# Weight parts in the weight's own column order, every fourth column as TensorE's stationary operand

## The reference, cut to what matters

```python
x = x + modulated(x, cond, w0)        # ((x * ys) @ w0) * d
x = x + rnn(x, h0=cond, Wx, Wh, b)    # h = tanh(h @ Wh + x @ Wx + b)
x = x + adapted(x, cond, base, ...)   # x @ (base + A_b B_b^T), A_b and B_b of rank 8, from cond
x = x + lstm(x, h0=cond, Wx, Wh, b)   # i, f, o, g of (x @ Wx + h @ Wh + b), 128 steps
```

## Time and profile before

| | |
|---|---|
| time, median of 3 runs | 1249.93 us (1248.52 to 1251.83) |
| the profiled execution | 1248.96 us, of which the span from the first to the last instruction is 1247.2 us |
| TensorE, matmuls | 1155.6 us busy, 93% of the span, 22740 matmuls and as many weight loads |
| VectorE | 877.9 us, 70% |
| ScalarE | 478.1 us, 38% |
| granted TensorE clock | 0.976 of full speed over the span |
| TensorE from 181 to 1140 us | 951.05 us busy of 959.00 |

### The profile page before, as it was taken

How to read it: one execution, slowest core, us unless ns; L and a number is a source line. 1 busy time by engine, 2 the same in 40 slices (tenths; PEclk the granted TensorE clock), 3 DMA queues, 4 the chain that set the end, 5 groups by cost and what they waited for, 6 DMA issues and landing times.

```text
span 1247.2 us, 50735 instructions
## 1 busy us (share of the span) xinstructions
PE 1155.6 (93%) x22740; PEld 755.4 (61%) x22740; DVE 877.9 (70%) x2483; ACT 478.1 (38%) x1148; POOL 55.4 (4%) x89
## 2 busy tenths in 40 slices
PE   4565699999999999999999999999999999999985
PEld 2452366666666666666666666666666666666642
DVE  6667577777777777777777777777777777776653
ACT  4366333334333333333433333333433333334332
POOL 1000000000000000000000000000000000000000
PEclk9787699999999999999999999999999999999999
DMA  8955000000000000000000000000000000000000
GB/s 301 369 217 161 1 16 9 17 19 20 20 19 20 19 20 9 13 20 20 20 20 19 20 20 12 12 18 20 20 19 20 19 20 19 10 4 11 11 11 18
DMA packets 49065, 51.00 MB, mean 41 GB/s; under 512 B 5984, under 2 KB 38752, under 8 KB 47184
## 3 DMA queue, kind: packets, MB, share of 16 engines
q1 hardware_dynamic: 48848, 47.77, 12.2%
HBM read 39.36 MB, written 8.39 MB: 38 GB/s over the span
## 4 chain that ended last, share of the span: by engine, by line
PE 46%; DVE 29%; ACT 14%; issue 9%; SPq 0%; DVEq 0%; ACTq 0%; DMA 0%; POOL 0%; POOLq 0%
PE ps_gates L1254 15%; PE ps_gates L1246 14%; PE ps_x L1186 7%; ACT rows L479 4%; PE ps_rnn L1270 3%; DVE gates_ring L935 3%; ACT gates_ring L581 2%; DVE lstm_hT L946 2%; PE ps_lr L1186 2%; DVE late L924 2%; PE ps_rnn L1273 2%; ACT x L479 2%; DVE x_ring L787 2%; PE ps_z L1186 2%; DVE x1T L751 2%
## 5 line engine op out<-in xcount | busy, mean ns | idle before, releaser
L1254 PE MATMUL ps_gates<-big,lstm_h 128*32 128x512 f16 x6144 | 355.0, 380 | 15.8 <-ACT lstm_h L479 15.6
L1246 PE MATMUL ps_gates<-big,rows 128*32 128x512 f16 x6144 | 355.8, 381 | 4.1 <-DVE rows L693 4.1
L1246 PEld LDWEIGHTS ps_gates<-big,rows 128*32 128x32 f16 x6144 | 165.1, 97 | 172.5 <-issue 6.7
L1254 PEld LDWEIGHTS ps_gates<-big,lstm_h 128*32 128x32 f16 x6144 | 152.5, 96 | 170.7 <-ACT lstm_h L479 23.3
L935 DVE SCALAR_TENSOR_TENSOR gates_ring<-ps_gates,tile_un,rows 128x256 f32<-128x256 f32 x256 | 111.5, 477 | 45.4 <-PE ps_gates L1254 45.4
L581 ACT ACTIVATE gates_ring<-gates_ring 128x256 f32<-128x256 f32 x128 | 53.4, 417 | 203.1 <-DVE gates_ring L935 203.1
L1270 PEld LDWEIGHTS ps_rnn<-rnn_h,wh_hi 128*128 128x128 f16 x2048 | 90.5, 96 | 59.3 <-issue 51.8
L1270 PE MATMUL ps_rnn<-rnn_h,wh_hi 128*128 128x64 f16 x2048 | 120.6, 192 | 4.6 <-DVE rnn_h L784 4.4
L1273 PE MATMUL ps_rnn<-rnn_h,wh_lo 128*128 128x32 f16 x2048 | 115.9, 177 | 0.0
L479 ACT ACTIVATE lstm_h<-lstm_hT,tile_g 128x128 f16<-128x128 f32 x128 | 51.4, 402 | 121.0 <-DVE lstm_hT L946 121.0
L1186 PE MATMUL ps_l<-xs,w_hi 128*128 128x128 f16 x1024 | 81.8, 225 | 14.2 <-DVE xs L693 14.2
(11 more groups left out here) (183 smaller groups left out, 1583.7 us busy)
## 6 DMA issues: line engine op xcount, KB each, us to landing
ring<-in_hw SPq DMA_DIRECT2D x16, 1024.0 KB, 8.5
xT_sb<-in_xT SPq DMA_DIRECT2D x128, 64.0 KB, 2.3
outT<-late SPq DMA_DIRECT2D x128, 64.0 KB, 2.1
big<-in_wx SPq DMA_DIRECT2D x5, 1024.0 KB, 7.8
big<-in_wh SPq DMA_DIRECT2D x5, 1024.0 KB, 13.7
big<-in_w SPq DMA_DIRECT2D x1, 1024.0 KB, 5.5
big<-in_hw SPq DMA_DIRECT2D x1, 1024.0 KB, 5.9
late<-in_base SPq DMA_DIRECT2D x1, 1024.0 KB, 19.1
```

What stands on the lines that cost most here:

```text
L1246: nc.tensor.matmul(ps_gates[t % 2][B * j:B * j + B, :], x16[:, part, k, at:at + B], wx3_part(w_part, k)[:, GW * j:GW * j + GW], start=(n = ...
L1254: last = nc.tensor.matmul(ps_gates[t % 2][B * j:B * j + B, :], lstm_h16[:, part, k], wh3_part(w_part, k)[:, GW * j:GW * j + GW], start=Fal ...
```

## The change

The fp16 parts are kept in the weight's own column order. ScalarE and VectorE read and write adjacent columns, and do each weight in two pieces of 1024 columns (two of the four k chunks each) instead of four of 512; B keeps its two pieces. The semaphore counts follow (2 per weight instead of 4). TensorE's stationary operand is now every fourth column of the 512 of a chunk: 128 fp16 values that lie 8 bytes apart. Nothing else is changed; sizes, buffers, the order of the work and the number of matmuls are as before.

```diff
-        def turned_chunk(w, oc):
-            return w[:, :, P * oc:P * oc + P]
-        def loaded_chunk(w, oc):
-            return w.rearrange("p (k q c) -> p k q c", k=KC, c=KC)[:, :, :, oc]
-        def turned_columns(x):
-            return x.rearrange("p (c q) -> p c q", c=KC)
         def columns(x):
             return x.rearrange("p (q c) -> p c q", c=KC)
+        def loaded(w):
+            return w.rearrange("p (k n) -> p k n", k=KC)
+        def flat(w):
+            return w.rearrange("p k n -> p (k n)")
...
-                    sp.wait_ge(w_lo_ready, KC * (k + 1))
+                    sp.wait_ge(w_lo_ready, 2 * (k + 1))
...
             def weight_high(w_hi, slot, s_w):
-                for oc in range(KC):
-                    high(turned_chunk(w_hi, oc), loaded_chunk(big[:, slot], oc), s_w).then_inc(w_hi_ready, 1)
+                for half in range(2):
+                    at = slice(half * KC // 2, (half + 1) * KC // 2)
+                    high(w_hi[:, at], loaded(big[:, slot])[:, at], s_w).then_inc(w_hi_ready, 1)
...
-                    high(turned_columns(b_hi[:, half]), columns(ps_b[half][:]), s_b).then_inc(b_hi_ready, 1)
+                    high(b_hi[:, half], ps_b[half][:], s_b).then_inc(b_hi_ready, 1)
...
             def weight_low(n, w_lo, w_hi, slot, s_w):
-                for oc in range(KC):
-                    dve.wait_ge(w_hi_ready, KC * n + oc + 1)
-                    low(turned_chunk(w_lo, oc), loaded_chunk(big[:, slot], oc), s_w, turned_chunk(w_hi, oc))\
-                        .then_inc(w_lo_ready, 1)
+                for half in range(2):
+                    at = slice(half * KC // 2, (half + 1) * KC // 2)
+                    dve.wait_ge(w_hi_ready, 2 * n + half + 1)
+                    low(flat(w_lo[:, at]), flat(loaded(big[:, slot])[:, at]), s_w, flat(w_hi[:, at])).then_inc(w_lo_ready, 1)
...
-            def chunks(w, at):
-                return [w[:, k, at:at + P] for k in range(KC)]
+            def chunks(w, oc):
+                return [columns(w[:, k])[:, oc] for k in range(KC)]
...
-                                             [[w[:, half, P * oc:P * oc + P]] for w in (b_hi, b_lo)],
+                                             [[columns(w[:, half])[:, oc]] for w in (b_hi, b_lo)],
...
-                        nc.tensor.matmul(ps_rnn[:, at:at + 2 * B], wh1_hi[:, k, P * oc:P * oc + P],
+                        nc.tensor.matmul(ps_rnn[:, at:at + 2 * B], columns(wh1_hi[:, k])[:, oc],
...
-                        last = nc.tensor.matmul(ps_rnn[:, at:at + B], wh1_lo[:, k, P * oc:P * oc + P], rnn_h16[:, k, 0],
+                        last = nc.tensor.matmul(ps_rnn[:, at:at + B], columns(wh1_lo[:, k])[:, oc], rnn_h16[:, k, 0],
```

More of the change, by code:

```diff
@@ L538, in base_high @@
                 act.wait_ge(base_scale_ready, 1)
-                for oc in range(KC):
-                    high(turned_chunk(base_hi, oc), loaded_chunk(late[:], oc), s_base).then_inc(base_hi_ready, 1)
+                for half in range(2):
+                    at = slice(half * KC // 2, (half + 1) * KC // 2)
+                    high(base_hi[:, at], loaded(late[:])[:, at], s_base).then_inc(base_hi_ready, 1)
             def b_high():
@@ L857, in base_low @@
             def base_low():
[L858 to L861, removed]
+                for half in range(2):
+                    at = slice(half * KC // 2, (half + 1) * KC // 2)
+                    dve.wait_ge(base_hi_ready, half + 1)
+                    low(flat(base_lo[:, at]), flat(loaded(late[:])[:, at]), s_base, flat(base_hi[:, at])).then_inc(base_lo_ready, 1)
             def b_magnitude(q):
@@ L898, in b_low @@
                     dve.wait_ge(b_hi_ready, half + 1)
-                    low(turned_columns(b_lo[:, half]), columns(ps_b[half][:]), s_b, turned_columns(b_hi[:, half]))\
+                    low(b_lo[:, half], ps_b[half][:], s_b, b_hi[:, half])\
                         .then_inc(b_lo_ready, 1)
@@ L1187, in split_product @@
                 return last
-            def chunks(w, at):
-                return [w[:, k, at:at + P] for k in range(KC)]
+            def chunks(w, oc):
+                return [columns(w[:, k])[:, oc] for k in range(KC)]
             def dense(psum, w_hi, w_lo, x16, outs):
                 for oc in outs:
-                    last = split_product(psum[:, TOK * oc:TOK * oc + TOK], (chunks(w_hi, P * oc), chunks(w_lo, P * oc)),
+                    last = split_product(psum[:, TOK * oc:TOK * oc + TOK], (chunks(w_hi, oc), chunks(w_lo, oc)),
                                          [[x16[:, part, k] for k in range(KC)] for part in range(2)])
@@ L1291, in _ @@
             unfolded(ps_l1, lambda k: folded[:, P * k:P * k + P]).then_inc(u_ps, 1)
-            pe.wait_ge(w_lo_ready, KC)
+            pe.wait_ge(w_lo_ready, 2)
             l0(0)
             w2_unit(0)
-            pe.wait_ge(w_lo_ready, 2 * KC)
+            pe.wait_ge(w_lo_ready, 2 * 2)
             l1(0)
             w2_unit(1)
-            pe.wait_ge(w_lo_ready, 3 * KC)
+            pe.wait_ge(w_lo_ready, 2 * 3)
             pe.wait_ge(h0_lo, 1)
@@ L1326, in _ @@
             w2_unit(12)
-            pe.wait_ge(base_lo_ready, KC)
+            pe.wait_ge(base_lo_ready, 2)
             x3_base(0, range(KC))
```

## The result

| | before | after |
|---|---|---|
| time, median of 4 runs | 1249.97 us (1248.52 to 1251.83) | 1263.65 us (1263.37 to 1265.02) |
| ratio, with its 95% interval | | 1.0111 (1.0093 to 1.0128) |
| span of the profiled execution | 1247.2 us | 1263.2 us |
| TensorE, matmuls | 1155.6 us | 1185.9 us |
| TensorE from 181 to 1140 us | 951.05 of 959.00 | 957.56 of 959.00 |

The forecast was 1244.2 us, faster; the kernel became 13.7 us slower. The time lies in the stated range only because the range reached over the slower rivals, and it lies between them: B ended at 1257 and C stood at 1369, so no rival had priced it. The last two lines of the table say where the difference is: the start-up part is 5.1 us shorter, as forecast, and the loop is 21.1 us longer.

What follows compares the result with a forecast made beforehand. TensorE's own pace was taken to bound the loop, the weight split the start-up. Split gains of 1.72 + 1.76 + 2.2 = 5.7 us, with nothing for the loads, gave a median of 1244.2 us; range 1241.5 to 1378.

Steps and rivals of the forecast that it cites:

- B: RNN and low-rank loads: small toll of 2.4 ns each, as in the fp32 pair; about 1255 us, chance 0.13.
- C: RNN and low-rank loads: memory sets each stepped load at about 54 ns, dense products hidden; +119.5, 1369 us, chance 0.24.
- part 2: TensorE's 9472 weight loads with the new address pattern: claimed to cost nothing.
- The 140 ns: Upper bound for a stepped 128-column fp32 load, 0.56 / 4, used to claim a far element every 1.1 ns or faster.
- the split's 5.7: Start-up gain in us from cheaper splitting on VectorE and ScalarE: w0 1.72, wx1 1.76, base 2.2.
- the 26 waits: TensorE's loop waits for ScalarE's lstm_h, 7.8 us in all, expected to give back up to 2.0 us under a small toll.
- an fp32 pair: Two products with the same fold matrix, stepped and adjacent: eight loads take 1.94 and 1.78 us, 9% more.
- ScalarE's ratio: ScalarE's fp32 reads at a step of four against none, 1.77 ns for 0.83; carried to weight loads, about 55 ns.
- D: All stepped loads, dense ones too: fast load lost altogether, 140 ns each; +923, so 2173 us, chance 0.08.
- E: Start-up part: loads cost nothing but the split's gain doesn't arrive in full; 1247 to 1251 us, chance 0.09.
- the 2 us allowed for the clock: Start-up part: allowance of 2 us either way on the gain, for TensorE's clock changing level several times.
- the 2.2 that were worked out: Start-up split of base: two high pieces on ScalarE instead of four let wh3 start earlier, gain 2.2 us.

Runs made afterwards that it cites:

- experiment 6: The kernel before with only the RNN's stationary operand read at a step of eight columns (16 bytes) over two chunks: 1369.8 us, ratio 1.0956.
- experiment 1: The changed kernel with TensorE taking 128 adjacent columns again, the cheaper split kept: 1241.47 us, ratio 0.9936 to the kernel before.
- the mixed one: The changed kernel with wh1 and B turned as before and loaded adjacent, w0, wx1 and base in own order: 1245.24 us, again 1245.06; ratio 0.9967 both times.

## Why the prediction was wrong

**The step that failed** is part 2, "I take nothing for the load". It was argued so: a stepped fp32 load fetches a far element every 1.1 ns or faster, a fp16 load brings one element per quarter every 0.84 ns, four quarters are loaded at once, and so a step of four is covered. Two things are wrong in it. The first can be seen in its own figures: 1.1 ns for each of the 32 elements of a quarter bounds the load at 35 ns, which leaves room for 8 ns over the 26.9 of an adjacent one, and 1.2 ns used up the gain of the split. The 1.1 was called "near" 0.84 where a seventh of the difference decided the sign. The measured pace, 33.4 ns, is 1.04 ns for each of 32 elements. The second is the premise that no row showed, that the four streams don't hinder each other. Where every element lies 16 bytes or more from the next, as in the fp32 load, it would again give at most 35 ns; measured were 60 (experiment 6), or 0.47 ns for each of 128 elements. That is 2.3 times as fast as the 1.1 ns of the fp32 load, not four times.

The 140 ns came from the length of four loads. The starts in the same trace are closer:

```profile
91.82 0.56 PEld L1166 LDWEIGHTS ps_x<-ident,rows 128*128 128x128 f32 x4
92.29 0.57 PEld L1166 LDWEIGHTS ps_lr<-ident,rows 128*128 128x128 f32 x4
```

0.47 / 4 = 117 ns for a load is 0.92 ns for an element and 29 ns for a quarter. By that, too, the sign was open, and the 33.4 ns of the step of four already lie above what four unhindered streams would need.

**The sum.** 4096 x 6.5 = 26.6 us for the RNN and 3.1 for the low rank are 29.7; less 8.1 that the waits gave back, less the gain of the split. Put into the forecast in place of nothing, with the split's 5.7, they give 1249.93 + 29.7 - 8.1 - 5.7 = 1265.8, and 1263.65 was measured. The forecast's own rule, an RNN pace over 28.1 ns makes it wrong in its sign, held.

**The rivals.** B had the right mechanism, places and hiding: a toll in the RNN and the low rank, none in the dense products, waits that shrink. Its size was off: 2.4 ns per load, carried over from an fp32 pair as 9% of 26.9 ns; 6.5 was measured. So was what the waits give back: it took one time step's toll for each of the 26 waits, which at 0.21 us would be 5.4 us, and from 200 to 1150 us they fell by 7.6. The fp32 loads of the earlier trace rows take 222 and 242 ns each, so they are held by something else, and their ratio said little. Their elements were 16 bytes apart, which was read as the harder case; in absolute terms that pair differed by 20 ns per load, and a fp16 load at the same spacing costs 33 ns more than an adjacent one (60 for 26.9). C is right in that the step alone can make the load far slower; that it is the memory which sets it is not shown, and at this step the pace is 33.4 ns and not 54. What C priced is nearly what a step of eight does (1369.8 us measured, 1369 worked out for C, a coincidence of the number). Among what spoke for C was ScalarE's ratio, which is of a 16-byte step and not of 8 bytes. D didn't happen at any step up to sixteen. In E's place: the gain of the start-up did arrive.

**The start-up part** was right in its pieces, and its sum came near partly by luck: w0's pieces took 1140 and 1278 ns where 1146 and 1284 were worked out, l1(0) at 35.29 for 35.4. The gain at the first LSTM step is 5.1 us for 5.7, and 8 RNN steps of 0.21 us more, 1.7 us, are part of that time. With adjacent columns the whole gained 7.6 us, 1.9 more than the 5.7, within the 2 us allowed for the clock; some 1.5 of it go with the clock, as said at experiment 1. The same kernel's first LSTM step moved by 1.4 us between two executions (141.01 and 139.64 us for the mixed one). wh3's first low part came 3.3 us earlier (111.16 for 114.50) and not 5.7. Of the 3.5 us of lead at l1(0) only 1.1 were left when VectorE began base's low part (108.23 for 109.34), and base gave the 2.2 that were worked out. Most of the lost lead went when l1(1) ran with a lower granted clock; the RNN steps' tolls took some of the rest. The windows of that product, in the changed kernel,

```profile
61.80:65.90 4.10, 4.09 (x49) 4.10 (x50) 0.42 (x2) 3.73 (x4) 0.19 (x1) 0.64 1.03 430
```

and in the kernel before:

```profile
64.40:67.20 2.80, 2.77 (x51) 2.77 (x52) 0.45 (x2) 2.71 (x3) 0.00 (x0) 1.00 1.01 421
```

The granted clock was 0.64 on average, half speed at first and full speed at the end (its groups of 12 took 1.26, 1.28, 0.87 and 0.67 us), where it had been 1.00 throughout, and the product took 4.1 us for 2.7. Later the clock gave part of this back: gates_x(0) took 4.14 us at 0.64 for 4.86 at 0.55.

**The pages.** The Trainium skill, page "TensorE: Matmul & The Clock Gate", section "Weight-path perf modes — Fast Weight Load (FWL) and DoubleRow", says that the fast load takes a packed or a stepped operand. The runs agree that it isn't lost (61.7 ns at most in the RNN, not 140), but not that a stepped one is as fast: it was 33.4 ns at a step of four. The page "Advanced Engine Details and Errata", section "Memory Cachelines", says that at least two hits on a 16-byte line are needed for the full rate. For VectorE this case agrees (pairs of fp32 columns, 1282 ns for 1282), for ScalarE nearly (1214 for 1140), and for weight loads it does not: two hits per line were the 33.4 ns, and it took four hits, a step of two, to keep 26.9. I had drawn from both that the loads cost nothing. Neither page gives a price for a stepped load or says what four streams do together.

**What stays open** is what limits the stepped load. The count of 16-byte pieces fits all five steps, but so would any limit that grows from 4 to 16 bytes of spacing and stops there: no run separates the number of pieces from the spacing, since every stationary operand tried here has a single step. If the four quarters are read at once, the distance between them grows with the step too, and no run holds it fixed. What sets 26.9 ns at steps of one and two isn't shown either: two patterns with one pace say that it need not be the reading of the weights. That the moving operand takes a share of the same limit would explain 63 to 64 ns beside 128 moving columns against 60 beside 32 and 64, and was not tested by itself.

## What to carry to other kernels

Ask of a changed operand what sets the pace of the instruction that reads it: the same stepped load was all but free behind 128 moving columns and cost 6.5 ns each, 25 us in all, where nothing but the load set the pace. A bound from one stream (fp32, one element at a time) doesn't carry over to a load that fetches several at once; when a term has 4864 instances and breaks even at 1.2 ns, "near" has to be worked out to that precision, and "no row shows it" should weigh more than a plausible chain of reasons. And when two orders of the data each favour one engine, look for one between them: pairs of columns kept both the cheap split and the fast load.

## What the runs showed of the hardware that was not expected

- Matmuls with 128-column fp16 weight loads, beside 32 or 64 moving columns, start 26.9 ns apart at steps of 1 and 2 elements, 33.4 at 4, 60.0 at 8 and 61.7 at 16.
- The dense products hide a load of 33.4 ns but for 0.36 ns behind 128 moving columns (0.673 us for 12 matmuls against 0.669), and one at a step of eight not: 62 to 65 ns each.
- ScalarE and VectorE read pairs of fp32 columns (8 of every 16 bytes) at 1214 and 1282 ns for 1024 elements, 1140 and 1282 for adjacent ones; every fourth column costs 1201 and 1112 ns for only 512.
